# Expert token weights of two mixtures: row loads from memory in place of products with a picking matrix, applied directly behind each item's product

## What is computed (reference, cut to what matters)

```python
# mixture 0: 8 experts of width 128, 2 chosen per token, and 2 blocks of 128 shared by all tokens
scores = softmax((x @ wt.T + repeat(g @ wg.T)) / 2)
topk_w, topk_idx = top_k(scores, 2); topk_w /= topk_w.sum(-1) + 1e-20
y_all = einsum(leaky(x @ w_gate[e]) * (x @ w_up[e]), w_down[e])      # for every expert
y = sum over the 2 chosen of topk_w * y_all  +  shared part (weight 1)
# mixture 1, on y: 16 experts of width 64, 4 chosen (from 2 of 4 groups), and 512 shared columns
scores = sigmoid(y @ router_w.T) ; w = chosen scores / their sum
out = sum w * (silu(y @ gate_w) * (y @ up_w)) @ down_w  +  shared part  (+ residual x1)
```

## Time and profile before

| what | value |
|---|---|
| median of 3 runs | 2709.37 us (2703.78 to 2712.18) |
| the profiled execution's own time | 2723.18 us |
| its span, first to last instruction | 2721.4 us |
| PE busy in the span | 2480.8 us (91%) |
| DVE busy | 1718.3 us (63%) |
| ACT busy, POOL busy | 1225.9 us (45%), 1333.3 us (49%) |
| the mixtures' part of the span | 1807.6 to 2721.4, that is 914 us |

### The profile page before, as it was taken

The page is one execution under the profiler, slowest core; times in us unless marked ns, Lnnn a source line. Parts: engine busy times, 40 slices in busy tenths (PEclk is TensorE's granted clock), DMA queues, the critical chain, the costliest instruction groups (busy, mean ns, idle before and its releaser), DMA issues. The chain is left out here.

```text
span 2721.4 us, 56667 instructions
## 1 busy us (share of the span) xinstructions
PE 2480.8 (91%) x20878; PEld 2049.2 (75%) x20926; DVE 1718.3 (63%) x4142; ACT 1225.9 (45%) x3095; POOL 1333.3 (49%) x1467
## 2 busy tenths in 40 slices
PE   5999999999999999579999999958899999999998
PEld 3788888888888888367877778846677777777776
DVE  4667776767676766566666665345756746756573
ACT  2666566666666665454444442123333233233332
POOL 3667676767676765365555554015422222222222
PEclk7999999999999999689888887768999999999999
DMA  4000100000000000011111222051000000000000
GB/s 135 7 10 9 43 17 10 13 10 9 10 9 9 7 7 5 16 37 21 51 42 44 53 52 53 25 139 43 8 16 8 16 11 22 16 9 16 16 1 24
DMA packets 136912, 71.49 MB, mean 26 GB/s; under 512 B 81920, under 2 KB 131584, under 8 KB 136592
## 3 DMA queue, kind: packets, MB, share of 16 engines
q1 hardware_dynamic: 131072, 62.83, 8.8%
q10 hardware_dynamic: 5568, 5.04, 0.6%
HBM read 47.35 MB, written 20.49 MB: 25 GB/s over the span
## 5 line engine op out<-in xcount | busy, mean ns | idle before, releaser
L1512 POOL TENSOR_TENSOR m_hid_part<-m_hid,m_hid_part 128x512 fp32r<-128x512 f32 x176 | 237.5, 1350 | 629.8 <-ACT m_hid_part L1440 628.9
L920 POOL TENSOR_TENSOR a_bm<-a_bias,a_mask_add 128x512 f32<-128x512 f32 (+3 forms) x512 | 437.6, 871 | 190.9 <-DVE a_nm L674 186.0
L830 ACT ACTIVATE a_S<-a_S,a_nm 128x512 f32<-128x512 f32 (+3 forms) x512 | 289.2, 565 | 346.8 <-DVE a_nm L674 344.0
L674 DVE CUSTOM_DVE_ANT_0 a_S<-a_S,a_bm,a_nsn 128x512 f32<-128x512 f32 (+3 forms) x512 | 275.5, 545 | 141.2 <-PE a_S L438 136.9
L461 PE MATMUL a_O<-a_v,a_PT 128*128 128x64 f32 x2560 | 342.6, 265 | 0.0
L461 PEld LDWEIGHTS a_O<-a_v,a_PT 128*128 128x128 f32 x2560 | 328.5, 193 | 0.1
L1400 PE MATMUL m_Y<-m_hid_part,m_down_high 128*128 128x512 f32 x704 | 274.4, 431 | 37.9 <-POOL m_hid_part L1512 37.8
L438 PE MATMUL a_S<-a_kT,a_qT 128*128 128x384 f32 (+3 forms) x1024 | 284.5, 359 | 3.5 <-DVE a_nm L674 3.0
L1440 ACT CAST m_hid_part<-m_hid 128x512 fp32r<-128x512 f32 x176 | 109.0, 619 | 326.9 <-DVE m_hid L1577 323.3
L1372 PE MATMUL m_G<-m_in,m_gate_high 128*128 128x512 f32 x704 | 251.7, 398 | 2.0 <-POOL m_up_low L1506 1.1
L1372 PE MATMUL m_U<-m_in,m_up_high 128*128 128x512 f32 x704 | 249.4, 395 | 0.0
(11 more groups left out here) (323 smaller groups left out, 5398.5 us busy)
## 6 DMA issues: line engine op xcount, KB each, us to landing
a_x<-in_x SPq DMA_DIRECT2D x32, 128.0 KB, 2.1
s_hT<-a_hT SPq DMA_DIRECT2D x32, 128.0 KB, 2.1
d_x<-in_x SPq DMA_DIRECT2D x8, 512.0 KB, 4.8
d_h<-s_hT SPq DMA_DIRECT2D x8, 512.0 KB, 4.3
s_xg<-d_xg SPq DMA_DIRECT2D x8, 512.0 KB, 3.0
d_x<-s_xg SPq DMA_DIRECT2D x8, 512.0 KB, 4.4
s_x<-d_x SPq DMA_DIRECT2D x8, 512.0 KB, 4.1
m_x_turn<-s_x SPq DMA_DIRECT2D x8, 512.0 KB, 3.8
```

Source lines behind the costliest of these rows:

```text
L674: dve.tensor_tensor_reduce(S[:, n % S_SLOTS, 0:w], SB[n % 2][:, 0:w], bm[:, n % BM_SLOTS, 0:w], -1.0, nsn[:, tile % 2, h:h + 1], ALU.add, ...
L830: act.activation(S[:, n % S_SLOTS, 0:w], S[:, n % S_SLOTS, 0:w], ACT.Exp, scale=-1.0, bias=nm[:, tile % 2, h:h + 1], accum_out=den[:, tile ...
L920: pool.tensor_tensor(bm[:, n % BM_SLOTS, 0:w], bias[:, h, L - w:L], mask_add[b % 2][:, 0:w], ALU.add).then_inc(s["bm_ready"], 1)
L1512: pool.tensor_tensor(hid_part[1][:, q % H_SLOTS], hid[:, q % G_SLOTS], hid_part[0][:, q % H_SLOTS].bitcast(F32), ALU.subtract).then_inc(hi ...
```

## The change

The bfloat16 parts, the picking matrix, its product and the bank `m_W` go. The float32 token weights are transposed as they are to `wT` (two copies, by the group's parity), written by ACT's queue to memory (`w_dram`, 32 KB at most), and for every expert item a row of 2 KB is loaded from there into all 128 partitions (for mixture 1 two rows, each into 64 partitions), into one of four slots of `spread`. `weigh(q)` moves from step q+1 to right behind `mult_up(q)` on DVE and reads the slot in SBUF. The steps of `weights` move, in mixture 0 from item 1 of the group to the last item of the group before (group 0: from step 2 to 0, group 1: from item 2 to item 0), in mixture 1 from item 2 to item 1 (group 2: from 3 to 2). Groups 0 and 1 get all three routing parts in one step. The routing of group 2 starts one step earlier. The wait for the late loads moves from q = 0 to q = -1.

In order, the pieces are: tiles; steps of the side work; PE (weights_turned, spread, start); ACT at the end of step q, before the outputs are taken; POOL; DVE (routing part weigh, weigh(q), the loop).

```diff
-        MB16 = MB[:, :].bitcast(BF16)
-        N_LATE = 3
+        N_LATE = 2
...
-        parts = sb("parts", [P, TT, 3 * E2], BF16)
-        wT = sb("wT", [P, L], BF16)
+        wT = [sb(f"wT{i}", [E2, L]) for i in range(2)]
+        W_SLOTS = 4
+        spread = sb("spread", [P, W_SLOTS, L])
...
-        route_from(0, -1)
+        PARTS[-1] = [(part, 0) for part in ("spread", "choose", "weigh")]
         for g, (m, b) in enumerate(GROUPS):
             q0 = FIRST[g]
-            side(q0 + (3 if g == 2 else 2 if g < 2 or m == 1 else 1), ("weights", g))
+            W_AT[g] = q0 + (0 if g < 2 else -1 if m == 0 else 2 if g == 2 else 1)
+            side(W_AT[g], ("weights", g))
             if g == 0:
...
-                route_from(1, q0 + N1 - 1)
+                PARTS[q0 + N1 - 1] = [(part, 1) for part in ("spread", "choose", "weigh")]
             elif m == 0:
-                at = 4 if b == 1 else 2
+                at = 3 if b == 1 else 2
...
+        W_LOADS = {}
+        for q in range(NQ):
+            if routed(q):
+                W_LOADS.setdefault(max(q - W_SLOTS + 1, W_AT[ITEMS[q][0]] + 1), []).append(q)
...
-                    n = 3 * NE[GROUPS[g][0]]
-                    pe.wait_ge(parts_ready, nth(("weights", g)))
+                    n = NE[GROUPS[g][0]]
+                    pe.wait_ge(w_ready, nth(("weights", g)))
...
-                        last = pe.transpose(MB16[0:n, t * P:(t + 1) * P], parts[:, t, 0:n], ident16[:])
+                        last = pe.transpose(MB[0:n, t * P:(t + 1) * P], w[:, t, 0:n], ident[:])
...
-                def spread(q):
-                    pe.matmul(WB[:, :], pick[:, m, item - SHARED[m]], wT[:], start=True, stop=True)\
-                      .then_inc(weight_psum, 1)
...
-                pe.wait_ge(wT_clean, 1)
...
+                    for step in SIDE.get(q, ()):
+                        if step[0] == "weights":
+                            act.wait_ge(wT_ready, nth(step))
+                            act.dma_start(w_dram[g % 2, 0:n], wT[g % 2][0:n]).then_inc(wT_out, 16)
+                    for at in W_LOADS.get(q, ()):
+                        g, m, b, item = ITEMS[at]
+                        slot = (n_routed(at) - 1) % W_SLOTS
+                        act.wait_ge(wT_out, 16 * nth(("weights", g)))
+                        if n_routed(at) > W_SLOTS:
+                            act.wait_ge(weighted, n_routed(at) - W_SLOTS)
+                        for e in range(1 + m):
+                            part = slice(e * M2, e * M2 + M2) if m else slice(0, P)
+                            one = w_dram[g % 2, (1 + m) * (item - SHARED[m]) + e, :]
+                            act.dma_start(spread[part, slot], bass.AP(tensor=one.tensor, offset=one.offset,
+                                                                      ap=[[0, part.stop - part.start], [1, L]]))\
+                               .then_inc(spread_in[slot], 16)
...
-                pool.memset(pick[:], 0.0).then_inc(zeroed, 1)
-                pool.memset(wT[:], 0.0).then_inc(wT_clean, 1)
...
+                        if g > 0:
+                            dve.wait_ge(wT_psum, g)
...
-                        link(dve.tensor_copy(parts[:, :, 0:n], wn))
-                        link(dve.tensor_tensor(r, wn, parts[:, :, 0:n], ALU.subtract))
-                        link(dve.tensor_copy(parts[:, :, n:2 * n], r))
-                        link(dve.tensor_tensor(r, r, parts[:, :, n:2 * n], ALU.subtract))
-                        dve.tensor_copy(parts[:, :, 2 * n:3 * n], r).then_inc(parts_ready, 1)
...
-                    dve.wait_ge(weight_psum, n_routed(q))
-                    dve.tensor_tensor(h, h, WB[:, :], ALU.mult).then_inc(weighted, 1)
+                    slot = (n_routed(q) - 1) % W_SLOTS
+                    dve.wait_ge(spread_in[slot], 16 * n_spread(q))
+                    dve.tensor_tensor(h, h, spread[:, slot], ALU.mult).then_inc(weighted, 1)
...
-                dve.tensor_copy(ident16[:], ident[:])
...
-                    if q == 0:
-                        dve.wait_ge(loaded_late, 16 * N_LATE)
-                        dve.tensor_copy(pick[0:3 * E2], pick_in[:])
...
                         dve.tensor_tensor(h, h, UB[q % 2][:, :], ALU.mult).then_inc(mult_up, 1)
+                        if routed(q):
+                            weigh(q)
...
-                            dve.tensor_copy(wT[0:n, :], MB16[0:n, 0:L]).then_inc(wT_ready, 1)
+                            dve.tensor_copy(wT[g % 2][0:n], MB[0:n, :]).then_inc(wT_ready, 1)
...
-                    if 0 <= q - 1 < NQ and routed(q - 1):
-                        weigh(q - 1)
...
+                    if q == -1:
+                        dve.wait_ge(loaded_late, 16 * N_LATE)
                     for part in PARTS.get(q, ()):
                         route(*part)
```

More of the change, by code:

```diff
@@ L1002, in rank_below, with mixtures_phase @@
     link(dve.tensor_scalar(out, out, float(k), None, ALU.is_lt))
-def mixtures_phase(nc, a, ident, mixture, shared_sems, x1_dram, out):
+def mixtures_phase(nc, a, ident, mixture, shared_sems, x1_dram, w_dram, out):
     F32R = mybir.dt.float32r
@@ L1134, in mixtures_phase @@
         exps_ready = sem("exps_ready")
-        parts_ready = sem("parts_ready")
+        w_ready = sem("w_ready")
         wT_psum = sem("wT_psum")
@@ L1139, in mixtures_phase @@
         up_psum = sem("up_psum")
-        weight_psum = sem("weight_psum")
+        wT_out = sem("wT_out")
+        spread_in = [sem(f"spread{i}_in") for i in range(W_SLOTS)]
         gate_active = sem("gate_active")
@@ L1256, in n_routed, with n_spread @@
             return sum(routed(j) for j in range(q + 1))
+        W_LOADS = {}
+        for q in range(NQ):
+            if routed(q):
+                W_LOADS.setdefault(max(q - W_SLOTS + 1, W_AT[ITEMS[q][0]] + 1), []).append(q)
+        assert all(at < qs[0] for at, qs in W_LOADS.items())
+        def n_spread(q):
+            return sum(1 + ITEMS[j][1] for j in range(q + 1) if routed(j) and (n_routed(q) - n_routed(j)) % W_SLOTS == 0)
         def n_y_act(g):
@@ L1440, in high @@
                     act.copy(hid_part[0][:, q % H_SLOTS], hid[:, q % G_SLOTS]).then_inc(hid_high, 1)
-                late = [(lower[:], a["c_lower"]), (cb[:], row(a["L0_ffn_correction_bias"], E2)), (pick_in[:], a["c_pick"])]
+                late = [(lower[:], a["c_lower"]), (cb[:], row(a["L0_ffn_correction_bias"], E2))]
                 assert len(late) == N_LATE
@@ L1480, in _ @@
                         high(q - 1)
+                    for step in SIDE.get(q, ()):
+                        if step[0] == "weights":
+                            g = step[1]
+                            n = NE[GROUPS[g][0]]
+                            act.wait_ge(wT_ready, nth(step))
[12 more added lines that the diff above has]
+                               .then_inc(spread_in[slot], 16)
                     g = taken_at(q)
@@ L1621, in _ @@
                             g = step[1]
-                            n = 3 * NE[GROUPS[g][0]]
+                            n = NE[GROUPS[g][0]]
                             dve.wait_ge(wT_psum, nth(step))
-                            if g == 0:
-                                dve.wait_ge(wT_clean, 1)
-                            else:
-                                dve.wait_ge(weight_psum, n_routed(FIRST[g] - 1))
-                            dve.tensor_copy(wT[0:n, :], MB16[0:n, 0:L]).then_inc(wT_ready, 1)
+                            dve.tensor_copy(wT[g % 2][0:n], MB[0:n, :]).then_inc(wT_ready, 1)
                         elif step[0] == "back":
@@ L2512, in bass_adaln @@
                         scratch["x1"])
-        mixtures_phase(nc, a, ident, mixture, sems, scratch["x1"], out)
+        mixtures_phase(nc, a, ident, mixture, sems, scratch["x1"], scratch["w"], out)
 def kernel(**inputs):
@@ L2532 @@
     arrays["c_lower"] = _np.ascontiguousarray(_np.broadcast_to(_np.tril(_np.ones((E2, E2), _np.float32), -1), (P, E2, E2)))
-    pick = _np.zeros((3 * E2, 2, 8, P), _np.float32)
-    for s in range(3):
-        for i in range(8):
-            pick[E1 * s + i, 0, i, :] = 1
-            for e in range(2):
-                pick[E2 * s + 2 * i + e, 1, i, M2 * e:M2 * (e + 1)] = 1
-    arrays["c_pick"] = pick
     arrays["c_cond"] = _np.ascontiguousarray(inputs["cond_64"].T)
```

25 lines of the change are left out of this document (6 added, 19 removed).

## The result

The changed kernel takes **2695.6 us** (median of 12 runs, 2684.2 to 2713.6), the kernel before 2709.1 beside it: ratio 0.995, interval 0.9927 to 0.9974, so 7 to 20 us less. That is faster by more than 0.3%, as forecast, but it is 13.5 us in place of 35.4. The figure lies in the range (2656 to 2700), the forecast 2674 doesn't stand.

The account below looks back on a forecast made before the run. PE was taken to bound the steady mixtures, something else the opening, with DVE-bound stretches making PE's holes. Gains 12.0 + 1.9 + 5.3 + 1.1 + 15.1 = 35.4 us off the median 2709.4 gave 2674, range 2656 to 2700.

Parts of the forecast that it names:

- Picking products: Where PE is the bound, outside the DVE-bound stretches: dropping these products saves 12.0 us over six runs of items.
- Stretches: Six DVE-bound runs of items beside mixture 1's routing (from items 36, 58, 80 and so on): earlier weigh gains 5.3 us.
- X: Start of mult_up(63) on DVE, in the stretch from item 58; item 67 was to start at X+14.2 against X+15.56.
- (d): Opening, group 1: PE's wait of 4.02 us moves two steps forward, shrinks to about 1, half-clock run goes: 6.4 us.
- Last group: Last mixture-1 group: 1.9 us from 8 picking products, 0.2 from routing stalls, with `weights` delayed by about 2.4.
- Tail: Behind the last item, weigh(175) follows mult_up at once: 0.9 us less (0 to 1.2).
- Opening: Start of the mixtures, up to about item 24: 15.1 us gained, the least certain sum, bounds 8 and 21.
- (a): Start: PE's first transposition no longer waits 3.10 us for the clearing of `pick` and `wT`: 2.8 us gained.
- DVE and POOL collide more: Rival 2, chance 0.18: POOL blocks weigh too in seven routing stretches, costing 22 us (2696) or 44 (2718).
- Rows come late: Rival 3, chance 0.07: weigh of each group's first expert items waits for its row; landing at 12 us costs 75 (2749).
- The start gives nothing: Rival 4, chance 0.08: POOL's splitting or the weights' landing takes up the opening's gain, leaving 22 us: 2687.
- the stretches give more: Rival 1, chance 0.12: L1563 isn't blocked and the start comes near its bound 21, gaining 48 us: 2661.

Follow-up runs that it names:

- e4: Changed kernel plus 13 idle PE products (8 in the last group) ahead of the wait at mixture 1's weights, from the fifth group on: 2684.9 us.
- e1: Changed kernel with every mixture-1 group's weights step in the group's item 2 instead of item 1: 2673.7 us.
- e7: Changed kernel with 2 slots for the rows instead of 4, so a row is loaded one item ahead of its weigh: 2691.0 us.
- e8: Changed kernel with the seven weight splits of items 9 to 15 moved to items 12 to 15, two an item: 2698.3 us.
- e3: Kernel before, keeping picking products, no row loads; weigh directly behind mult_up, groups 0 and 1 routed in one piece, their weights in item 0: 2699.9 us.
- e6: e1 with mixture 1's routing, from the fifth group on, begun five steps earlier and its DVE operations dealt out over 12 steps by a budget: 2664.5 us.
- e9: e6 with mixture 1's two turns in items 3 and 4 instead of 2 and 3, and a budget of 1.5 us instead of 1.3: 2655.4 us.
- e10: e9 with splits of items 9 to 11 moved to 12 to 14, and idle PE products ahead of the waits at weights: 2662.4 us.

## Why the prediction was right in its direction and wrong in its size

*Picking products*: right. 11.3 for 12.0; items of 4.21.

*Stretches*: the step that failed. "PE, done with item 65 at X+3.7, waits until then" was right to 0.1 us (3.62 measured), and "X+7.4" for L1575's semaphore too. The sentence behind it, "From there: transpositions 0.6, m_Y(63) 1.5, item 66 with turn 0.44: 4.64", put the full clock behind a wait of 3.7 us. m_G(67) started at X+15.21, not X+14.2. From mult_up(58) it is 44.91, which is over the 44.7 that I had named as a sign of being wrong. In the earlier trace rows stood the counterexample: 4.02 us of wait, then clock 0.50. I used it under (d) as something that goes, and not here as something that comes, six times over. e4 prices it: 9.1 of the 10.7 us by which the six stretches missed. With the clock kept up the stretch from item 58 takes 46.78, and the forecast was 46.7 (47.73 less 1.0). In the changed kernel X itself came 0.6 late (29.7 behind mult_up(58), not 29.1), by the 0.12 a step of a dependent operation; the 0.4 that I had taken off for a collision of weigh covers most of it.
The Trainium skill has the rule (TensorE: Matmul & The Clock Gate, The HAM clock gate): the low rate is the array's default, and activity releases it; the windows above agree, 0.50 behind the idle time. I didn't draw on it.

The larger omission is not a number. I took the place of weights as given and priced the wait that it makes, without asking what it would be an item later. e1 shows that the wait wasn't needed: 21 us lay in it.

*Last group*: 0.4 for 2.1, with 2.40 of wait at weights as forecast ("about 2.4"). Behind it the granted clock is 0.50 in the changed kernel (2631 to 2633), and items 166 and 167 take 8.19 and 4.77. In e7 and e8, whose last group has the same steps and the same wait of 2.40, it is 1.00 (2633 to 2637), the two items take 7.20 and 4.2, and the gain would be 2.0. So the forecast holds in two executions of three, and the difference is the clock again. *Tail*: 0.9, right.

*Opening*: (a) 3.1 for 2.8; up to m_G(3) 7.9 for 7.4; up to m_G(10) 8.9 for 8.9. Then (d) failed: "moves two steps forward and shrinks to about 1" became 3.34, and the clock behind it is 0.73 and then 0.70 (1864 to 1870), and up to m_G(15) the gain was 11.4 for 15.7. The routing of group 1 was made in one piece, and I took it without POOL; e8 shows 2.7 us of the chain to be waiting for the weight splits. How much of the 4.3 us is due to this can't be said closely: items 0 to 15 range over 2.4 us in executions of the same code. The last 0.7 of the 5.0 lie in items 15 to 23, where I took 0.6 off and 1.3 went.

*Rivals*. "DVE and POOL collide more": not through weigh. Of 128 weighs, 59 took over 0.72 us, most of them 0.80 to 0.83 and ten 1.2 to 1.7, 15.4 us in excess; but none of these lies in the steps that DVE bounds (items 59 to 63 in the period shown), and the ones of 1.67 lie in items of 4.2, where PE was busy throughout. The Trainium skill's rule (SBUF — State Buffer, Who interferes with whom) is borne out by e3, whose 128 weighs with a PSUM operand took 0.69 at most; but taken as a price for this change, as the second rival did, it gave 22 to 44 us that weren't paid. "Rows come late": excluded, since even with half the slots (e7) the waits cost PE nothing. "The start gives nothing" and "the stretches give more": neither, as the rows stood. That a *wait which the change moves* could cost more than all its holes had was among none of my cases.

*The comparison*: I took the same gain off both numbers, and that was right only for the mixtures; the profiled executions differ by 16 us more in stages that are the same.

## What to carry to other kernels

Removing a wait in front of an engine brings only what its next wait leaves: price the arrival (here 3.6 us early) and the clock behind it, and then try the neighbour step for what the engine now meets too early. Two places that act on the same engine are tried in all four combinations: here the direct weigh was 10.7 us worse or 15.6 better, and the later weights 19.4 better or 6.9 worse, each by the other. Where two steps share a bank, look for the wait that this makes before placing them side by side (e6 and e9). When an engine is overloaded in some steps and idle in others, deal its operations out by the step's spare time: from e1 to e9 that was worth 18 us by the medians (15 by the profiled mixtures), as much as the change itself.

## What was unexpected in the hardware

- A DVE operation that reads what the one before it wrote, and waits for its semaphore, started 0.72 us behind it, an independent one of the same size 0.60, with either SBUF or PSUM as its other operand.
- Idle products in an unused bank made a kernel faster: 3.2 us of them in a wait of 3.6 saved 1.2 to 2.5 us behind it (e4). Where PE had no wait, three of them cost 0.7 us (e10).
- The same wait in the same code isn't always followed by the lower clock: behind 2.40 us in the last group the granted clock was 0.50 in the changed kernel and 1.00 in e7 and e8; behind 1.82 us ahead of `rows` (item 75 and its like) it fell in all six places in e9 and in two of six in e6.
- A DVE operation on 128x32 with one tensor operand (L1002) took 1.81 us beside POOL's 128x1024 subtraction, ten times its usual 0.18. I had counted only operations with two SBUF operands as open to this. The Trainium skill says of tensor_scalar that it can contend with GpSimd (SBUF — State Buffer, Who interferes with whom).
- The same wait after the same code ranged from 1.7 to 4.9 us between executions (item 10), which makes one wait of the opening a poor measure.

What stays open: why the low clock lasts some 3 us behind one wait of 3.62 and over 5 behind another of the same length, and why it follows a wait of 2.40 in one execution and not in another; no run here varies that alone. Why items 9 to 11 differ by 2 us between executions of the same code wasn't tried either.
